# Four-layer GNN stack: incidence rows and adjacency transposed by DMA, five incidence rows made during layer 0

## What is computed

```
L0:  gt = adj.T;  y = D gt D (h @ W0) + bias          D = diag(rowsum(gt) ** -0.5)
L1:  head = (adj > 0);  head = head / sqrt(rowsum(head * head))
     inc = adj + head;  y = (inc @ h) / rowsum(inc)
L2:  ht = (h @ W2) in 4 heads of 256;  e = leaky_relu(src_i + dst_j) + adj_ij
     y = mean over heads of softmax_j(e) @ ht
L3:  y = relu(adj @ (relu(sign(h)) @ sign(W3).T))
```

## Time and profile before

| | us |
|---|---|
| median of 3 runs (754.66 to 756.65) | 754.7 |
| the profiled execution | 754.57 |
| its span, first to last instruction | 752.8 |
| load stage | 0 to 70 |
| layer 0 on PE | 70 to 157 |
| layer 1 (last product taken) | to 304.3 |
| scores and ht blocks | to 350 |
| 16 groups of layer 2 | to 690 |
| layer 3 and the stores | to 752.8 |

### The profile page before, as it was taken

One profiled execution on the slowest core, in us unless ns is written; L12 is line 12 of the kernel. 1 busy time (PEld: TensorE's weight loads), 2 busy tenths in 40 slices (PEclk: granted clock), 3 DMA queues, 4 the chain that ended last, 5 costly groups with the idle time before them and its releaser, 6 DMA issues.

```text
span 752.8 us, 16841 instructions
## 1 busy us (share of the span) xinstructions
PE 731.1 (97%) x6816; PEld 622.8 (83%) x6816; DVE 648.9 (86%) x1196; ACT 485.9 (65%) x893; POOL 62.6 (8%) x102
## 2 busy tenths in 40 slices
PE   4999999999999999999999999999999999999998
PEld 3665888898889999546888888888888888888887
DVE  6788896868888886489999999999999999997683
ACT  4897020277677775587655877768696886766751
POOL 3004120211111110000000000000000000000000
PEclk7898999999999999999999999999999999999999
DMA  8886590055556633775011812135111713126691
GB/s 330 302 297 226 80 236 17 2 173 212 206 212 232 232 150 141 236 175 166 1 30 32 241 25 42 29 81 172 30 30 29 204 50 58 25 64 194 224 391 57
DMA packets 44173, 105.98 MB, mean 141 GB/s; under 512 B 3072, under 2 KB 17984, under 8 KB 39616
## 3 DMA queue, kind: packets, MB, share of 16 engines
q1 hardware_dynamic: 39824, 94.94, 36.4%
q0 software_dynamic: 4272, 9.96, 7.9%
HBM read 78.12 MB, written 18.91 MB: 129 GB/s over the span
## 4 chain that ended last, share of the span: by engine, by line
PE 83%; DVE 8%; ACT 6%; DMA 2%; issue 1%; SPq 0%; DVEq 0%; ACTq 0%
PE ps L746 15%; PE ps L747 15%; PE ps L748 15%; PE ps L686 4%; PE ps L788 3%; PE ps L789 3%; PE ps L582 3%; PE ps L581 3%; PE ps L580 3%; PE ps L609 3%; PE ps L633 2%; PE ps L635 2%; PE ps L634 2%; PE ps L613 2%; ACT arena L823 2%; DVE arena L1260 2%
## 5 line engine op out<-in xcount | busy, mean ns | idle before, releaser
L746 PE MATMUL ps<-arena 128*128 128x257 f16 x1024 | 280.0, 273 | 0.0
L748 PE MATMUL ps<-arena 128*128 128x257 f16 x1024 | 279.4, 273 | 0.0
L747 PE MATMUL ps<-arena 128*128 128x257 f16 x1024 | 279.3, 273 | 0.0
L1070 ACT ACTIVATE arena<-arena 128x512 f16<-128x512 f32 x252 | 158.5, 629 | 93.9 <-PE ps L748 61.9
L1393 DVE SCALAR_TENSOR_TENSOR arena<-arena,w_j 128x512 f32<-128x512 f32 x256 | 190.1, 744 | 0.0
L1400 DVE TENSOR_TENSOR arena<-arena 128x512 f16<-128x512 f32 x256 | 175.6, 687 | 3.7 <-ACT arena L1070 3.5
L747 PEld LDWEIGHTS ps<-arena 128*128 128x128 f16 x1024 | 100.3, 98 | 12.6
L748 PEld LDWEIGHTS ps<-arena 128*128 128x128 f16 x1024 | 99.8, 97 | 13.0
L746 PEld LDWEIGHTS ps<-arena 128*128 128x128 f16 x1024 | 99.9, 98 | 12.7
L633 PE MATMUL ps<-arena 128*128 128x257 f16 x256 | 70.3, 275 | 0.0
L635 PE MATMUL ps<-arena 128*128 128x257 f16 x256 | 69.7, 272 | 0.0
(11 more groups left out here) (154 smaller groups left out, 1183.8 us busy)
## 6 DMA issues: line engine op xcount, KB each, us to landing
arena<-in_adj_dram SPq DMA_DIRECT2D x32, 512.0 KB, 5.8
arena<-in_adj_dram SPq DMA_DIRECT2D x16, 1024.0 KB, 5.1
adj_t<-arena SPq DMA_DIRECT2D x16, 1024.0 KB, 5.5
arena<-adj_t SPq DMA_DIRECT2D x64, 256.0 KB, 4.1
arena<-adj_t SPq DMA_DIRECT2D x16, 1024.0 KB, 6.5
x<-arena POOLq DMA_DIRECT2D x15, 512.0 KB, 4.8
arena<-u_rows SPq DMA_DIRECT2D x4, 1024.0 KB, 13.6
x<-in_x_dram SPq DMA_DIRECT2D x4, 512.0 KB, 5.8
```

The source lines that it names most:

```text
L746: mm(ps[:, bank, 0:DE], hi, ht_hi[:, head, j, 0:DE], start=s, stop=False)
L747: mm(ps[:, bank, 0:DE], hi, ht_lo[:, head, j, 0:DE], start=False, stop=False)
L748: ins = mm(ps[:, bank, 0:DE], lo, ht_hi[:, head, j, 0:DE], start=False, stop=e)
L1070: nc.scalar.activation(p_hi[:, j % 4, :], prob[:, j % 4, :], copy).then_inc(p_hi_done, 1)
```

## The change

The turned incidence rows and the turned adj no longer come from PE. SP writes the 16 MB of `nat` to DRAM once at the start of layer 0. For layer 1 the incidence row is split in its natural layout (`inc_high` on ACT, `inc_low` on DVE) and turned by two DMA transposes of 512 KB (`turn_inc`). Five sets of turned rows (`AHEAD`) and four accumulator banks replace two and two; five rows are filled and four of them split during layer 0. For layers 2 and 3 SP turns 512 x 512 blocks of the float16 parts from DRAM (`turn_adj`, 16 pairs, two slots), and POOL writes each to DRAM as float32 by a casting DMA (`widen_high`) and an accumulating one (`add_low`). The row buffers are three instead of four. POOL's partition_all_reduce of the maximum moves behind layer 0, `exp_adj` of the first quarter behind the first ht blocks, and the layer-3 splits of rows 0 and 1 from quarters 1 and 2 to the last quarter.

The diff, cut to its core:

```diff
+        COUNTS = (1, 2, 8, 9, 11, 13)
+        FILLS = (3, 4, 10, 11, 13)
+        HIGHS = (4, 7, 11, 12, 15)
+        LOWS = (5, 8, 12, 14)
+        AHEAD = 5
+        WIDEN_AFTER = {0: (6, 7), 4: (8, 9), 5: (10, 11), 8: (12, 13), 9: (14, 15)}
+        SENT = ((0, 1), (1, 3), (3, 5), (5, 8), (8, 11), (11, NB))
-        ACC = (0, 2)
+        ACC = (1, 3, 4, 5)
...
+            def reload_rows(t):
+                sp.wait_ge(filled, t - 2)
+                load_rows(t)
+            def turn_inc(t):
+                sp.wait_ge(inc_lo_done, t + 1)
+                if t >= AHEAD:
+                    sp.wait_ge(l1_ps, t - AHEAD + 1)
+                for part in range(2):
+                    sp.dma_start_transpose(out=inc_parts[t % AHEAD][:, part, :, :], in_=inc_nat[t % 2][:, part, :]
+                                           ).then_inc(inc_in[t % AHEAD], 16)
+            def turn_adj(n):
+                q, g = n // TG, n % TG
+                if n >= 2:
+                    sp.wait_ge(wide[(n - 2) % TG], 16 * ((n - 2) // TG + 1))
+                slot = (turn_l1 if q == 0 else turn_l2)[:, n % 2]
+                for part in range(2):
+                    sp.dma_start_transpose(out=slot[:, part, :, :],
+                                           in_=nat_dram[TG * P * g:TG * P * (g + 1), part, QB * P * q:QB * P * (q + 1)]
+                                           ).then_inc(turned[n % 2], 16)
             sp.wait_ge(nat_lo_done, HALVES)
             for t in range(2):
                 load_rows(t)
-            sp.wait_ge(y_ps, 5)
...
+            for k, (lo, hi) in enumerate(SENT):
+                for b in range(lo, hi):
+                    sp.dma_start(nat_dram[b * P:(b + 1) * P], nat[:, b, :, :, :].rearrange("p a j n -> p a (j n)")
+                                 ).then_inc(nat_sent[k], 16)
+            reload_rows(3)
+            reload_rows(4)
+            sp.wait_ge(y_ps, 6)
+            sp.wait_ge(max_made, 7)
+            sp.wait_ge(nat_sent[3], 48)
+            load_rows(2)
...
+            for t in range(2, NB):
+                if t < AHEAD:
+                    sp.wait_ge(y_ps, 10 + t)
+                turn_inc(t)
+                if t + 5 < NB:
+                    reload_rows(t + 5)
...
+            for n in range(QB):
+                turn_adj(n)
             def load_e(q):
-                for b in range(2):
-                    sp.wait_ge(adjt_sent[b], 16 * 2 * (q + 1))
                 for g in range(NB // TG):
+                    sp.wait_ge(wide[g], 16 * (q + 1))
...
             for q in range(1, NQ):
+                for g in range(TG):
+                    turn_adj(QB * q + g)
+                if q == NQ - 1:
+                    for g in range(TG):
+                        sp.wait_ge(wide[g], 16 * NQ)
+                    for i in range(2):
+                        sp.dma_start(adjt_early[i], adjt_dram[i]).then_inc(adjt_in[4 + i], 16)
                 load_e(q)
...
+            def widen_high(n):
+                pool.wait_ge(turned[n % 2], 32 * (n // 2 + 1))
+                nc.gpsimd.dma_start(wide_rows(n), turned_slot(n)[:, 0, :, :]).then_inc(wide_hi, 16)
+            def add_low(n):
+                pool.wait_ge(wide_hi, 16 * (n + 1))
+                nc.gpsimd.dma_start(wide_rows(n), turned_slot(n)[:, 1, :, :], accum_op=ALU.add
+                                    ).then_inc(wide[n % TG], 16)
             for t in range(NB):
-                if t + 3 < NB:
-                    inverse_count(t + 3)
+                if t + 6 < NB:
+                    inverse_count(t + 6)
                 if t >= 1:
                     inverse_root2(t - 1)
+                if t == NB - 1:
+                    widen_high(0)
             inverse_root2(NB - 1)
+            add_low(0)
+            for n in range(1, QB):
+                widen_high(n)
+                add_low(n)
...
             for t in range(NB):
+                if t >= 2:
+                    h2_turned(t - 2)
+                if t + 6 < NB:
+                    count(t + 6)
+                if t >= 1:
+                    h2_high(t - 1)
+                if t + 5 < NB:
+                    inc_high(t + 5)
...
             for t in range(NB):
                 if t >= 1:
                     row_sums(t - 1)
                     row_norm(t - 1)
+                if t + 4 < NB:
+                    inc_low(t + 4)
+                if t + 6 < NB:
+                    make_mask(t + 6)
+                if t + 5 < NB:
+                    fill(t + 5)
                 if t >= 1:
                     h2_low(t - 1)
```

More of the change, by code:

```diff
@@ L219, in gnn_stack @@
         slot_in = [sem(f"slot_in{k}") for k in range(SLOTS)]
-        rows_in = [sem(f"rows_in{k}") for k in range(4)]
+        rows_in = [sem(f"rows_in{k}") for k in range(3)]
+        nat_sent = [sem(f"nat_sent{k}") for k in range(6)]
         bias_in = [sem(f"bias_in{p}") for p in range(4)]
@@ L266, in gnn_stack @@
         inc_lo_done = sem("inc_lo_done")
-        adjt_copied = sem("adjt_copied")
-        adjt_sent = [sem(f"adjt_sent{b}") for b in range(2)]
+        inc_in = [sem(f"inc_in{k}") for k in range(5)]
+        turned = [sem(f"turned{b}") for b in range(2)]
+        wide_hi = sem("wide_hi")
+        wide = [sem(f"wide{g}") for g in range(NB // TG)]
         l1_ps = sem("l1_ps")
@@ L410, in load_adjt @@
                              ).then_inc(adjt_in[k], 16)
-            for b in range(2):
-                sp.wait_ge(adjt_sent[b], 16 * NB // 2)
             for k in range(4):
@@ L500, in _ @@
                                     ).then_inc(head_added, 16)
+                for n in WIDEN_AFTER.get(group, ()):
+                    widen_high(n)
+                    add_low(n)
         @block.tensor
@@ L951, in _ @@
             h2_turned(NB - 1)
-            for j in range(4):
-                exp_adj(0, j)
             act.wait_ge(d_shift, 1)
@@ L967, in ht_high @@
             def ht_high(t):
-                if t == 0:
-                    for b in range(2):
-                        act.wait_ge(adjt_sent[b], 16 * NB // 2)
                 for h in range(HEADS):
```

282 lines of the change are left out of this document (113 added, 169 removed).

## The result

The changed kernel takes 824.7 us in the median of four runs (821.5 to 829.6), the kernel before 755.1 us beside it: a ratio of 1.092 (95% interval 1.086 to 1.099). The forecast was 794 us, slower, in a range of 757 to 845. The profiled execution has a span of 820.7 us against 752.8.

A forecast was written before the change was run, and what follows sets the result against it. PE was taken to bound the kernel, with DVE's and DMA waits replacing it after the change. Layer 1's end +8, u +19 and last quarter +12 gave +39 on 754.6, so 794 us, range 757 to 845.

The forecast's parts named there:

- if nothing else moved: Layer 1: PE without its 32 transposes a tile saves 3.5 us on each of 15 tiles, some 50 us.
- DVE's iteration: Layer 1: DVE's work and its wait for h2_high replace PE's 9.25 us a tile as the pace, at 9.9 us.
- The wait for row 2: Layer 0: row 2 queues behind 16 MB of stores, landing at 134; DVE stands 15 us (3 to 23).
- Free up to about 12 us: Layer 1: a pair of incidence-row turns, taken as 8 us, costs nothing up to about 12 us.
- the h2_low wait: Layer 1: DVE's h2_low waits for h2_high and inverse_root2 behind the next count, 4.2 us from mask's end, 2.26 hidden.
- The side case of a lower clock: Layer 1: PE's granted clock falling to 1.2 GHz makes a tile 11.4 instead of 5.7 us, up to 15 us in all.
- Before layer 2: Between layer 1 and first numerators: u_bc waits behind four turned, widened and added blocks, shifting layer 2 by 19 us (6 to 25).
- the +40: Before layer 2: the time after layer 1's end taken for block 3 to be done, between +24 and +44.
- Last quarter: Layer 2: SP waits for all 16 blocks before loading e, so ACT and PE wait 12 us (0 to 20).
- B: Rival: DVE's wait for h2_low doesn't come and row 2 lands by 122, giving 739 us; chance 0.14.
- C: Rival: DMA transposes take more than 12 us a pair; at 16 us, 845 us in all; chance 0.21.
- A: The forecast itself: the three waits hold and transposes are no bound; 794 us, bounds 760 to 820; chance 0.61.

The follow-up runs named there:

- the run with the roots first: Kernel after, with layer 1's row-norm root on POOL and h2_high on ACT ahead of the count's root and count: 815.5 us, ratio 1.080 to before.
- three other orders: Kernel after, layer 0 queue reordered: last eight stores behind row 2, 826.3 us; also bias first, 824.1; stores interleaved plus layer 1 and last-quarter reorders, 791.1.
- the run with e first: Kernel after, with SP issuing the last quarter's e loads before waiting for all 16 blocks and loading two adj rows: 804.8 us, ratio 1.068 to before.

## Why the prediction was right, and where it was off

**What bounds the kernel.** The reading that some 50 us would go "if nothing else moved" was wrong, and it was wrong on rows that looked complete: a chain mostly PE (83% of it, not "nearly all"), a tile of 9.25 us full of matmuls. Taking away half of that work, 1.75 us of PE a tile, gave 3.1 us in all of layer 1, where the reading gives 26. The chain didn't show a second ring of equal length. It did no harm to the sum, because that went by DVE's iteration.

**Layer 0.** Row 2 landed at 137 (134 forecast, 122 to 142), DVE left at 185.0 (182), but by two pieces where one was forecast. The first tile was 9.5 us late, since the bias took 37.2 us in the median to land instead of 18.8: the prediction had put 4 us of contention on row 2 and none on the bias. The wait for row 2 was then 9.3 instead of 15. Another place in the queue for row 2 was no cure: three other orders had the reduce within 6 us of 182.7, half the bytes of the stores at 167.1.

**Layer 1.** Iteration 9.7 for 9.9 (10.3 with a piece of `w2_lo`), layer 1's end 314.2 for 312, the idle of 1.9 us ended by ACT as forecast, and its cause (the roots behind the counts) shown by the run with the roots first. "Free up to about 12 us" for a pair of turns was too generous: with the h2_low wait gone, pairs of some 7.4 us already cost DVE 1.1 us of idle a tile. The side case of a lower clock didn't cost: the granted clock was 0.86 in 182 to 314, between its levels of 1.2 and 2.4 GHz after the gaps of PE, but DVE waited for ACT there and not for PE, and the tail of the layer, at a granted clock of 1.00 from 290 on, goes at 5.67 us a tile for the 5.75 forecast (303.03, 308.69, 314.36).

**Before layer 2.** The mechanism is right, the term is mis-sized: +32 for +19. Up to the widening of block 2 the chain kept to the forecast (done at 339.6, +25.5 for +26). Then the turn of block 3 landed only at 346.7, its widening took until 357.4 (10.7 us for 6.5), and with an add of 8.5 it was there at +52; the working had come to +44 and the prediction had taken +40 without a reason. From there to the first numerators it was 14 us for 13. So of the 13 us missing, some 4 are the turn of block 3, 4 its widening, 4 the +40 and 1 the rest. Without the add the stage is 22 us shorter.

**Last quarter.** Right in place, mis-sized again: +26.1 for +12. The accumulate of group 9 came 3 us later than the shift so far explains (613.8), the two rounds took 33.4 us (to 647.2) instead of 25, the e loads 12.9 to the first exponential (660.0) instead of 10. The SP order, e behind the wait for all 16 blocks, is shown as the cause for 18 of the 26 us by the run with e first. Not forecast: 4 us in group 7, where the prediction gave earlier quarters "a group or more to spare".

**Rivals.** B (the covers hold) fell with the wait for h2_low and row 2; C fell with the plain copies. A's own bounds, 760 to 820, were passed by 5 us. The range holds only because its upper end, 845, was set by C, whose mechanism isn't what happened: that part is luck. The forecast is right in direction and in where the time goes, and gives little more than half of the loss (+39 of +68).

## To carry to other kernels

Before work is moved from a busy engine to DMA, take it away without replacement and look whether the interval moves; here PE was busy for 99% of layer 1, and 1.75 us less of its work a tile left the interval as it was. Count the bytes that the move adds to a stage and the serial landings in its chain (here turn, widen, add for each block): if a reordering only shifts the wait to the next load, it is the amount that has to shrink. And size a chain by the durations that such transfers take next to each other (10.7 us for a widening whose median is 7.3), not by their medians alone.

## What the runs showed of the hardware

- A DMA transpose of 512 KB (fp16) lands 5.2 us after its issue in the median within SBUF and 6.0 from DRAM; the Trainium skill (DMA: Bandwidth & Descriptors, Latency and other measured facts) has 261 GB/s for such a transpose, by which a pair would be 4 us by my estimate. Here a pair in layer 1 was issued in 7.2 to 8.5 us, so the measured number is nearly twice that estimate.
- With plain copies in place of the transposes, the same bytes at the same 193 GB/s showed a DMA share of 0.59 instead of 0.93 in the window of layer 1. In these two kernels the share goes with the number of small packets (under 512 B: 4608 and 136704), not with the bytes.
- A transpose was held at its issue while earlier transfers of its queue were open. The first one behind the stores and row 2 took SP 17.9 us, from 119.0 to 136.9, and DVE had row 2 at 137.1; a plain copy in its place was issued in 0.6 us. All four turns there took 26.3 us, and 32.2 behind eight more stores.
- Writing a turned block to DRAM from POOL, 1 MB as float32, took 7.3 us with a cast and 8.5 us with an accumulate in the median of 16, up to 10.5 and 11.0.
